# A graph attention layer: TensorE's hand-overs signalled by drains, and the gathers' lead raised from 4 groups to 14

## The reference

```python
sent  = nodes[senders] @ Ws + Ws_b                 # 4 heads of 32
e_att = sent + edges @ We + We_b
recv  = nodes[receivers] @ Wr + Wr_b
logits = mish(e_att + recv) @ attn_w + attn_b      # one for each head
w = exp(logits - segment_max(logits, receivers)[receivers])
w = w / segment_sum(w, receivers)[receivers]
out_nodes = segment_sum(w * e_att, receivers)
return layernorm(x + out_nodes)
```

## Time and profile before

| what | us |
|---|---|
| median of 3 runs (2175.09 to 2179.09) | 2175.18 |
| span of the profiled execution | 2661.8 |
| PE, DVE, ACT, POOL busy in it | 1917.4, 1895.0, 1927.7, 1575.1 |
| granted TensorE clock over it | 0.835 |

### The profile page before, as it was taken

How to read it: one execution, slowest core, us unless ns; L and a number is a source line. 1 busy time by engine, 2 the same in 40 slices (tenths; PEclk the granted TensorE clock), 3 DMA queues, 4 the chain that set the end, 5 groups by cost and what they waited for, 6 DMA issues and landing times.

```text
span 2661.8 us, 45397 instructions
## 1 busy us (share of the span) xinstructions
PE 1917.4 (72%) x13621; PEld 1789.2 (67%) x13621; DVE 1895.0 (71%) x3941; ACT 1927.7 (72%) x3126; POOL 1575.1 (59%) x1640
## 2 busy tenths in 40 slices
PE   5667777777776777776776777776777777776776
PEld 5567666766666776766666766666667676666665
DVE  2676777777777767776676777766777777677766
ACT  1777777777777777777777777777777777777774
POOL 2666656656666665666566656656666666556661
PEclk8888888888888887888888888878888888878877
DMA  6422322322232322232232232232223232223220
GB/s 191 130 77 80 105 83 78 112 79 77 81 111 77 97 96 77 77 113 79 76 112 79 78 105 86 78 100 90 78 93 99 79 98 95 77 86 104 79 79 17
DMA packets 106714, 240.18 MB, mean 90 GB/s; under 512 B 45800, under 2 KB 72546, under 8 KB 99658
## 3 DMA queue, kind: packets, MB, share of 16 engines
q1 hardware_dynamic: 53334, 132.54, 14.6%
q0 software_dynamic: 52224, 107.06, 14.1%
q10 hardware_dynamic: 1128, 0.25, 0.0%
HBM read 229.98 MB, written 9.74 MB: 90 GB/s over the span
## 4 chain that ended last, share of the span: by engine, by line
DVE 36%; PE 20%; another core or an unknown queue 18%; issue 17%; ACT 7%; DVEq 1%; DMA 1%; ACTq 0%; SPq 0%
PE ps_sum L827 7%; DVE Z L1122 6%; DVE tbuf L1138 6%; DVE tbuf L1129 6%; DVE Z L1205 5%; PE ps_z L815 4%; PE ps_z L816 4%; DVE onehot L1113 4%; DVE logit L1144 2%; PE ps_edgeT L793 2%; ACT tbuf L933 1%; ACT tbuf L930 1%; ACT tbuf L936 1%; ACT tbuf L923 1%
## 5 line engine op out<-in xcount | busy, mean ns | idle before, releaser
L717 POOL DMA_INDIRECT landing<-xs_table,src_i x1632 | 1574.2, 965 | 1034.1 <-issue 448.3
L815 PE MATMUL ps_z<-we_sb,edgeT 128*128 128x128 f32 x3264 | 767.2, 320 | 83.3 <-issue 82.4
L816 PE MATMUL ps_z<-xr_buf,onehotT 128*128 128x128 f32 x3264 | 751.9, 315 | 72.3 <-issue 71.5
L827 PE MATMUL ps_sum<-Z,onehot 128*128 128x132 f32 x3264 | 558.9, 321 | 204.7 <-DVE att L1224 95.2
L815 PEld LDWEIGHTS ps_z<-we_sb,edgeT 128*128 128x128 f32 x3264 | 613.0, 232 | 100.9 <-issue 97.3
L816 PEld LDWEIGHTS ps_z<-xr_buf,onehotT 128*128 128x128 f32 x3264 | 609.4, 231 | 83.1 <-issue 82.8
L827 PEld LDWEIGHTS ps_sum<-Z,onehot 128*128 128x128 f32 x3264 | 485.6, 224 | 223.8 <-issue 149.4
L1113 DVE TENSOR_TENSOR onehot<-iota_f,ps_dve 128x512 f32<-128x512 f32 x408 | 276.0, 677 | 432.5 <-remote 352.6
L923 ACT ACTIVATE tbuf<-Z,c_zmax 128x512 f32<-128x512 f32 x408 | 296.2, 726 | 165.7 <-DVE Z L1122 85.9
L907 ACT COPY edgeT<-ps_edgeT 128x512 f32<-128x512 f32 x408 | 235.3, 577 | 229.4 <-remote 179.9
L798 PE MATMUL ps_onehotT<-ident_half,onehot 128*128 128x128 bf16 x1632 | 176.6, 232 | 241.8 <-issue 103.8
(11 more groups left out here) (110 smaller groups left out, 1228.3 us busy)
## 6 DMA issues: line engine op xcount, KB each, us to landing
landing<-in_edge_attr_dram SPq DMA_DIRECT2D x51, 2048.0 KB
landing<-xs_table,src_i POOLq DMA_INDIRECT x1632
x_in<-in_x_dram SPq DMA_DIRECT2D x51, 64.0 KB
xr_in<-xr_table SPq DMA_DIRECT2D x51, 64.0 KB
out_dram<-y_out SPq DMA_DIRECT2D x51, 64.0 KB
xr_buf<-xr_table SPq DMA_DIRECT2D x50, 64.0 KB
xs_table<-onehot SPq DMA_DIRECT2D x2, 896.0 KB
xr_table<-landing SPq DMA_DIRECT2D x1, 1568.0 KB
```

Source lines behind the costliest of these rows:

```text
L717: nc.gpsimd.indirect_dma_start(gath[b][:, t, :], None, xs_dram, bass.IndirectOffsetOnAxis(ap=src_i[:, b, t:t + 1], axis=0))\
L815: nc.tensor.matmul(ps_z[q][:, j, :], edgeT[:, q, j, :], we_sb[:, :], start=True, stop=False)
L816: mm = nc.tensor.matmul(ps_z[q][:, j, :], onehotT[:, q, j, :], xr_buf[:, b, :], start=False, stop=True)
L827: mm = nc.tensor.matmul(ps_sum[:, 0:ZC], OHv[:, b, t, :], Zv[:, b, t, :], start=(t == 0), stop=(t == T - 1))
```

## The change

The constant `AHEAD` goes from 4 to 14. In `turn`, `products` and `sums` the increment no longer hangs on the last transpose or matmul; a separate `drain` instruction follows the batch on PE and carries it. There are four of them in a group, 1632 in all. PE's two other hand-overs (L835, L842) stay as they are.

```diff
-AHEAD = 4
+AHEAD = 14
@@ turn
                 for j in range(n):
-                    tr = nc.tensor.transpose(ps_edgeT[g % 2][:, j, :], edge_buf[:, b, a + j, :], ident[:, :])
-                tr.then_inc(edgeT_ps, 1)
+                    nc.tensor.transpose(ps_edgeT[g % 2][:, j, :], edge_buf[:, b, a + j, :], ident[:, :])
+                pe.drain().then_inc(edgeT_ps, 1)
...
-                tr.then_inc(onehotT_ps, 1)
+                pe.drain().then_inc(onehotT_ps, 1)
@@ products
-                    mm = nc.tensor.matmul(ps_z[q][:, j, :], onehotT[:, q, j, :], xr_buf[:, b, :],
-                                          start=False, stop=True)
-                mm.then_inc(z_ps, 1)
+                    nc.tensor.matmul(ps_z[q][:, j, :], onehotT[:, q, j, :], xr_buf[:, b, :],
+                                     start=False, stop=True)
+                pe.drain().then_inc(z_ps, 1)
@@ sums
-                mm.then_inc(sum_ready, 1)
+                pe.drain().then_inc(sum_ready, 1)
```

More of the change, by code:

```diff
@@ L797, in turn @@
                 for j in range(n):
-                    tr = nc.tensor.transpose(ps_onehotT[:, j, :].bitcast(BF16)[:, 0:P],
-                                             halves(OHv[:, b, a + j, :]), ident_half[:, :])
-                tr.then_inc(onehotT_ps, 1)
+                    nc.tensor.transpose(ps_onehotT[:, j, :].bitcast(BF16)[:, 0:P],
+                                        halves(OHv[:, b, a + j, :]), ident_half[:, :])
+                pe.drain().then_inc(onehotT_ps, 1)
             def products(w, b, k, g):
@@ L826, in sums @@
                 for t in range(a, a + n):
-                    mm = nc.tensor.matmul(ps_sum[:, 0:ZC], OHv[:, b, t, :], Zv[:, b, t, :],
-                                          start=(t == 0), stop=(t == T - 1))
-                mm.then_inc(sum_ready, 1)
+                    nc.tensor.matmul(ps_sum[:, 0:ZC], OHv[:, b, t, :], Zv[:, b, t, :],
+                                     start=(t == 0), stop=(t == T - 1))
+                pe.drain().then_inc(sum_ready, 1)
             def ends_to_row(w, b):
```

## The result

The changed kernel takes 2226.1 us (2224.7 to 2227.7, 4 runs) against 2175.1. The ratio is 1.0235, interval 1.0221 to 1.0250. It is slower, as forecast, but by 51 us and not by 125.

What follows compares the result with a forecast made beforehand. POOL's gathers bound the kernel before; with the drains PE becomes the bound. Start 70.8, 51 windows of 42.1 us, the end's 37.4 and a constant (47.8 less about 3) give 2300 us, range 2200 to 2510.

Steps and rivals of the forecast that it cites:

- What bounds the kernel before: POOL's gathers set the time: 1.248 us each, 39.9 to 40.5 us a window, ahead of ACT and DVE.
- The drains: On PE, 0.36 us a drain, 11.5 us a window, plus 1.2 for the sequencer: PE's window 40.6 us at full clock.
- The two bounds of one drain: A drain costs PE at least 0.16 us and at most, at half clock, some 0.5 us.
- A sign that didn't come: In the profile after, POOL waits for `z_ps` throughout the steady state, 14 groups ahead, with PE busy or draining.
- The sum: PE's chain: T = 153 + 51 x P, including the end's 37.4 us and a constant; P = 42.1 gives 2300.
- the 15.1 us: Gate 4 to 14: POOL's idle 15.45 us at the start shrinks by 15.1, if POOL stays the bound.
- The clock: PE's mean clock in timed runs taken as 0.96; the window becomes 41.8 us, 42.1 with a remainder of waits.
- Recording slows this program: Profiled execution 2661.8 us against 2175.2 timed; most of POOL's 549.1 us of waits for `z_ps` taken as recording's burden.
- Hidden drains: Rival: drains under 0.32 us keep PE below POOL and the start's 15.1 us are gained: 2160 us; chance 0.25.
- No change: Rival: drains hidden, the gathers' gain eaten because DVE or ACT is the real bound: 2175 us; chance 0.06.
- The late hand-overs: Rival: PE's late hand-overs to ACT also exist in timed runs and a drain cures them: some 2130 us; better still, 0.02.
- The clock that stays down: Rival: with gaps in every batch PE does too little at half clock to be raised: over 2510 us; chance 0.12.

Runs made afterwards that it cites:

- e6b: Kernel before with three gathers a group instead of four from the third window on: 2060.1 us, ratio 0.9472.
- e8: Kernel before with the second input of DVE's L1129 taken from PSUM (attention row) instead of Z in SBUF: 2125.2 us, ratio 0.9784.
- e3_z_only: Kernel before with one drain a group, behind the products, AHEAD at 4: 2176.1 us, ratio 1.0016.
- e4_turn_only: Kernel before with the two drains in `turn`, behind edge and one-hot transposes, AHEAD at 4: 2174.5 us, ratio 1.0002.
- e1: Kernel before with AHEAD = 14 alone, all increments still on matmuls: 2171.95 us against 2173.14, ratio 0.9994.
- e10_three: Kernel before with three drains a group (products and both in `turn`), sums signalling by their last matmul, AHEAD at 4: 2179.1 us, ratio 1.0032.
- second profile of the kernel before: Kernel before, unchanged, profiled again where it takes about 2173 us: 2175.2 us, span 2174.4, ratio 1.0010.
- e2: Changed kernel with AHEAD back at 4, the four drains alone: 2226.36 us, ratio 1.0249 to the kernel before.
- the fifth drain: Changed kernel with a fifth drain a group, mid-products, signalling nothing, on a chip where the kernel before takes 2648.3 us: 3307.7 us, ratio 1.248.
- e5b_five_drains: Changed kernel with a fifth drain in each group, mid-products, signalling nothing, where the kernel before took 2175.8 us: 2355.2 us, ratio 1.0825 to the kernel before.
- e6_fewer_before: Kernel before with three gathers a group from the third window on, on a chip where the kernel before takes 2648.3 us: 2290.2 us, ratio 0.863.

## Why the direction was right and the size wrong

**What bounds the kernel before: right.** POOL's gathers do (e6b, e8), ahead of ACT and DVE. With a quarter of the gathers gone a window still takes (2020.2 - 58.8) / 407 x 8 = 38.6 us, near the 37 to 38 that the prediction read for ACT and DVE.

**The drains: right in mechanism, and near in price.** Forecast were 0.36 us a drain and 1.2 us a window for the sequencer, so 12.7 us a window; the timeline shows 1.67 x 8 = 13.4. PE's window was forecast at 40.6 at full clock and 42.1 with 1.2 for the clock and 0.3 for a remainder of waits; measured are 41.75. That this is so close is partly luck: the drains took 0.7 more, and clock and waits together 41.75 - 27.9 - 13.4 = 0.45 instead of 1.5. That a drain ends when the matmuls before it have ended was read from one drain; in the profile after, the 406 drains behind the products that ran at full clock all end 0.295 to 0.297 us after the start of the last matmul, which takes 0.275 us, so 0.02 us after its end (0.05 by the prediction).

The two bounds of one drain were estimates from the earlier trace rows. The lower, 0.16 us, holds: at full clock the next batch behind the products starts 0.35 us after the last matmul instead of 0.11, 0.24 us more. The upper, 0.5 us at half clock, holds behind the products and just fails behind the edges' transposes. PE's timeline at half clock, first e3_z_only, then e4_turn_only:

```profile
977.99 0.64 PE L816 MATMUL ps_z<-xr_buf,onehotT 128*128 128x128 f32 x2
978.71 1.11 PE L793 MATMUL ps_edgeT<-ident,landing 128*128 128x128 f32 x4
```

```profile
482.52 1.06 PE L793 MATMUL ps_edgeT<-ident,landing 128*128 128x128 f32 x4
483.91 0.54 PE L798 MATMUL ps_onehotT<-ident_half,onehot 128*128 128x128 bf16 x4 [0.33 <-issue]
```

With the beat of 0.21 the last product starts at 978.20 and the last transpose at 483.16, so the next batch starts 0.51 us and 0.75 us later: 0.30 and 0.54 us over the beat, with what the sequencer does behind the drain. The medians in these two traces are 0.50 and 0.75.

**A sign that didn't come.** POOL was to wait for `z_ps` throughout the steady state. In the profile after it waits 22.6 us in all, and its gathers run from 38.6 to 2120.7 at (2120.7 - 38.6) / 1631 = 1.277 us each, 40.9 us a window. PE's window is only 0.9 us longer, so in 51 windows POOL gets some 45 us ahead, about 9 groups, and the gate lets it go 14. The experiments, not this wait, show that PE is the bound.

**The sum: the step that failed.** "I keep them as a constant", it said of 47.8 us that POOL's chain left of the time before, and it carried 44.8 of them over to PE's chain. They were no constant. They belonged to POOL: its last gather starts at 2135.7 and not at the 2089.1 of the sum, 46.6 us later. Its gathers take 1.287 us each on the mean and not 1.248, 63 us over the span, mostly because L1129 stretches some of them; against that stand the 15 us that POOL doesn't lose at the start. PE's chain has no such term; of it only 1.9 us lie outside the span. The first profile had a hint of it:

```profile
L717 POOL DMA_INDIRECT landing<-xs_table,src_i x1632: 938/944/1522, 38.4 to 2609.0; - x182
```

By its page these 1632 gathers are busy 1574.2 us, and 1632 x 0.944 = 1540.6. So 34 us of stretched gathers could be read there, and belonged into POOL's pace.

The start failed with it: PE's chain begins at 57.05 and not at 70.8, since the earlier trace rows come from an execution whose prologue was slow as well. The sum with what was measured, forecast first:

| term | forecast | measured |
|---|---|---|
| start of the products | 70.8 | 57.05 |
| 51 windows to the last add | 2147 | 2184.8 - 57.05 = 2127.7 |
| from the last add to the end | 37.4 | 2223.9 - 2184.8 = 39.1 |
| carried over | 44.8 | 1.9 |
| sum | 2300 | 2225.8 |

Of the 74 us too much, 43 are the constant, 14 the start, 19 the window and -2 the end. The comparison with the bound of before was off in the same way: PE's 41.75 had to be held against 40.9 and not against 39.9 plus an unknown.

**AHEAD: the 15.1 us were wrong**. The forecast of 2300 didn't use them, since with PE as the bound they were no gain. The gap of the earlier trace rows came from the slow prologue; in e1 the gate is worth 0.

**The clock: wrong in direction.** I forecast that gaps in every batch would lower it (0.96, or far less in a rival). It rose from 0.915 to 0.992. Before, PE ran through its batches and then stood for up to 2 us for ACT's copy and up to 3 us for the maxima. The traces, each between 120 and 2100 us, hold the following (e10_three is described above; half clock is a granted clock of 0.50):

| | kernel before | e10_three | after |
|---|---|---|---|
| pauses of PE over 1 us | 226 | 53 | 0 |
| longest pause, us | 3.62 | 2.61 | 0.91 |
| all pauses, us | 436 | 331 | 356 |
| stretches at half clock | 67 | 38 | 0 |
| us at half clock | 311 | 150 | 0 |
| granted clock | 0.92 | 0.96 | 1.00 |

In these three runs the clock goes with the long pauses and not with all idle time: e10_three stands idle for less than the changed kernel and still falls to half clock 38 times. No run changed the pauses alone, so this is a reading and not a test. The traces record the clock in steps of 3.4 us. In the second profile of the kernel before PE is busy for at most 0.56 of the step ahead of each of the 67 falls. The rival's reason, that PE could do too little at half clock to be raised again, is seen there too: PE is busy for 0.92 or more of the last step of each stretch, and for 0.24 to 0.91 of the 24 steps after which the clock stays at half. One such stretch, in the columns of the earlier trace rows:

```profile
348.10:351.50 3.40, 0.81 (x6) 0.52 (x4) 3.30 (x7) 3.12 (x5) 2.49 (x4) 0.51 0.15 39
351.50:354.90 3.40, 3.40 (x16) 3.40 (x17) 3.40 (x11) 2.61 (x4) 2.79 (x3) 0.50 0.16 41
355.00:358.40 3.40, 3.31 (x33) 3.12 (x32) 3.22 (x8) 3.33 (x7) 2.49 (x4) 1.00 0.18 52
```

The changed kernel has gaps in every batch and no fall in that time. The mean of 0.84 in the earlier trace rows was a trait of the slow execution.

**"Recording slows this program": wrong**, and the root of the errors in the start, in AHEAD and in the clock. The 487 us between the span and the median were taken for a burden of recording.

**The rivals.** Hidden drains fail by e2 and by the drain's length, but only just: three drains are all but hidden (e10). No change fails by the result, and ACT and DVE are not the bound before (e6b). The late hand-overs of the earlier trace rows are not in the second profile of the kernel before, whose POOL waits 18.4 us for PE, and drains cure nothing (e3, e4). The clock that stays down is not seen here. On the slow chip the fifth drain took the program to 3308 us at a mean clock of 0.798, so there some of that rival may be true; the changed kernel itself was not run there, and this stays open, as does why that chip is slower.

No version tried beats the kernel before with the reference's results. e8 shows where 49 us lie: an input of L1129 in PSUM. I have not tried it with the right data; the kernel's eight PSUM tensors are all in use.

## What to carry to other kernels

A drain on PE cost next to nothing here as long as PE's pace, drains and sequencer included, stayed below that of the engine that sets the time. So add up that pace first: here three drains a group cost 5 us in 2175 and the fourth 47. A remainder between a chain of work and the measured time belongs to that chain; don't carry it to another one before it is known what it is. The pace of an engine is its mean distance over the span where it waits for nobody, and not the best stretch. And if a profiled span is far from the timed runs, no start, wait or clock of it is a number for the sum; only distances in undisturbed stretches are.

## What the runs showed of the hardware

- A drain on PE ended about 0.3 us after the last matmul's start: in the profile after, the drain of the products lasts 1.97 us from 1302.9, and the last matmul starts at 1304.58. The next matmul started 0.35 us after the last one, where the beat is 0.11; with waits behind the drain it was up to 0.6 us (1341.53 to 1342.16). At half clock it was 0.50 us where the beat is 0.21 (e3_z_only).
- The beats behind a drain were slower: two took 0.32 us instead of 0.22 (e5b_five_drains).
- PE's increment on a matmul cost nothing here: in the second profile of the kernel before the edges' transposes start 0.11 us after the last product, the beat within the batch. Moved to a drain it cost 0.42 us each time, in PE's own time.
- Gathers that overlap DVE's L1129, with both inputs in SBUF, lasted up to 1.53 us instead of 0.94, 201 of 549 over 1 us (second profile of the kernel before). With one of the inputs in PSUM it was 4 of 529, and the kernel took 49 us less (e8_psum_before).
- The mean clock rose from 0.915 to 0.992 when PE's pauses became many and short: those over 1 us went from 226 to none.
- The kernel before took 2173 to 2176 us on three chips and 2648 us on a fourth. In e6_fewer_before, run there, PE stops within a batch, where nothing is waited for:

```profile
1308.58 0.27 PE L816 MATMUL ps_z<-xr_buf,onehotT 128*128 128x128 f32 x1 [0.22 <-issue]
1310.00 0.27 PE L816 MATMUL ps_z<-xr_buf,onehotT 128*128 128x128 f32 x1 [1.15 <-issue]
```
